# A chunked state-space layer with a mixture of experts on one core: the softplus and the spreading of the step sums move to GpSimd

## The reference

```python
h = quantised_table[x]                                   # 64 x 128 tokens, 192 wide
zxbcdt = layernorm(h) @ in_proj_w.T
dt = softplus(zxbcdt[..., -6:] + dt_bias)                # 6 heads
A_cum = cumsum(dt * -exp(A_log), axis=tokens)
Lmat = exp(A_cum[..., :, None] - A_cum[..., None, :])    # lower triangle
Y = (C @ B.T * Lmat) @ (x * dt) + D * x                  # per head
h = h + sigmoid(gate) * (rmsnorm(Y * silu(z)) @ out_proj_w.T) + layernorm(h)
out = h + experts(layernorm(h))
```

## Time and profile before

| | us |
|---|---|
| median of 3 runs | 1089.92 (1089.62 to 1092.22) |
| the profiled execution | 1093.7 |
| its span, first to last instruction | 1091.9 |
| TensorE busy | 941.4 |
| VectorE busy | 692.4 |
| ScalarE busy | 583.9 |
| GpSimd busy | 526.2 |

### The profile page before, as it was taken

One profiled execution on the slowest core, in us unless ns is written; L12 is line 12 of the kernel. 1 busy time (PEld: TensorE's weight loads), 2 busy tenths in 40 slices (PEclk: granted clock), 3 DMA queues, 4 the chain that ended last, 5 costly groups with the idle time before them and its releaser, 6 DMA issues.

```text
span 1091.9 us, 20110 instructions
## 1 busy us (share of the span) xinstructions
PE 941.4 (86%) x5743; PEld 613.0 (56%) x5744; DVE 692.4 (63%) x2047; ACT 583.9 (53%) x1195; POOL 526.2 (48%) x622
## 2 busy tenths in 40 slices
PE   0688898888988998898998879899989988889985
PEld 0234455455544554455455556677767666667774
DVE  3678998999989989899889433676651211212120
ACT  2657886778868777788675244233232232232330
POOL 6222435356354463551514427333447776775453
PEclk9889998999989899899897799999999999999997
DMA  4910011011101110010001212134331121222220
GB/s 107 319 43 10 16 44 42 5 46 45 44 3 45 44 47 30 18 45 30 25 9 55 66 33 77 51 98 123 112 83 47 53 61 43 55 59 70 69 59 22
DMA packets 50001, 61.53 MB, mean 56 GB/s; under 512 B 22525, under 2 KB 41689, under 8 KB 49413
## 3 DMA queue, kind: packets, MB, share of 16 engines
q0 software_dynamic: 16704, 30.54, 9.8%
q1 hardware_dynamic: 28580, 24.93, 7.5%
q10 hardware_dynamic: 4640, 5.13, 1.7%
HBM read 36.24 MB, written 25.92 MB: 57 GB/s over the span
## 4 chain that ended last, share of the span: by engine, by line
PE 40%; DVE 25%; issue 13%; ACT 12%; POOL 7%; DMA 2%; POOLq 1%; DVEq 0%; ACTq 0%
DVE xbc L1435 11%; PE cx L1219 6%; PE mm L1057 5%; PE yb L1219 4%; PE mm L1061 4%; PE mm L1207 4%; PE mm L1203 4%; PE sg L1203 3%; POOL out_dram L611 2%; PE sg L975 2%; DVE mix L1455 2%; ACT rows_s L747 2%; ACT h L694 2%; ACT xbc L722 2%; POOL list_u L576 1%
## 5 line engine op out<-in xcount | busy, mean ns | idle before, releaser
L1435 DVE SCALAR_TENSOR_TENSOR xbc<-mm,cw,xbc 128x508 f32<-128x508 f32 (+2 forms) x231 | 168.5, 741 | 31.8 <-ACT xbc L722 26.4
L1057 PE MATMUL mm<-xt_a,win_a 128*128 128x512 f32 x248 | 148.1, 681 | 35.7 <-DVE xbc L1435 26.7
L903 ACT ACTIVATE ht<-mm,b1s 128x256 f32<-128x256 f32 x102 | 44.7, 472 | 230.5 <-PE sg L1207 228.0
L592 POOL DMA_INDIRECT xg<-hr_dram,ids x80 | 81.3, 1016 | 80.3 <-DVE res L1762 44.3
L511 POOL TENSOR_TENSOR ybuf<-ybuf,zs 128x384 f32<-128x384 f32 x64 | 69.5, 1087 | 100.5 <-DVE ybuf L1468 100.5
L722 ACT ACTIVATE xbc<-mm,cb,cw 128x512 f32<-128x512 f32 x77 | 56.6, 775 | 108.6 <-PE mm L1061 108.6
L611 POOL DMA_INDIRECT out_dram<-osb,ids_s x80 | 81.7, 1021 | 64.3 <-DVE osb L1772 43.0
L1772 DVE TENSOR_TENSOR osb<-cx,res 128x192 f32<-128x192 f32 x40 | 14.2, 356 | 143.6 <-PE cx L1219 142.0
L1203 PE MATMUL mm<-fx_a,w1a_t 128*128 128x256 f32 x240 | 81.9, 424 | 13.7 <-issue 7.6
L1219 PE MATMUL cx<-w2s,ht 128*128 x408 | 86.8, 365 | 5.5 <-issue 5.2
L1207 PE MATMUL mm<-fx_b,w1b_t 64*128 64x256 f32 x240 | 85.3, 436 | 0.0
(11 more groups left out here) (273 smaller groups left out, 2068.6 us busy)
## 6 DMA issues: line engine op xcount, KB each, us to landing
hr_dram<-hr SPq DMA_DIRECT2D x16, 768.0 KB
w2s<-in_w2c_dram SPq DMA_DIRECT2D x4, 576.0 KB
w2s_u<-in_w2u_dram ACTq DMA_DIRECT2D x4, 576.0 KB
list_c<-fill SPq DMA_DIRECT2D x2, 1032.0 KB, 12.3
list_u<-fill SPq DMA_DIRECT2D x2, 1032.0 KB, 18.5
w1a<-in_w1c_dram SPq DMA_DIRECT2D x4, 384.0 KB
w1a_u<-in_w1u_dram ACTq DMA_DIRECT2D x4, 384.0 KB
xg<-hr_dram,ids POOLq DMA_INDIRECT x80, 3.1
```

The source lines that it names most:

```text
L592: nc.gpsimd.indirect_dma_start(out=xg[:, v, t, :], out_offset=None, in_=rows, in_offset=bass.IndirectOffsetOnAxis(ap=ids[:, v, t, 0:1], ax ...
L1057: mmul(tile_bank(g2, m)[:, :], win_a[:, column(m):column(m) + P], xt_a[:, p, :], start=True, stop=False)
L1435: ins = stt(out=dst_[:, :, back:L], in0=src[:, :, 0:L - back], scalar=cw[:, m, TAPS - 1 - back:TAPS - back], in1=dst_[:, :, back:L], op0=A ...
```

## The change

Two pieces of work go to GpSimd. ScalarE keeps `rows_t` and makes one row more, `rows_u` (the sums, or 1, in all blocks), earlier than before: ahead of `start(6)` and `start(7)`. GpSimd multiplies `rows_u` by a mask in `seg_c` and so fills `rows_s` in two halves (`spread_rows(0)` and `spread_rows(1)`), and `seg(j)` waits for the half that it needs. VectorE keeps the first two operations of the softplus (`soften`) and does them ahead of `residual(0)`; the other ones of the series and the four writes of `drep` are done by GpSimd, twelve operations in place of eight, since the fused ones are split.

```diff
@@ gpsimd
+                def spread_rows(q):
+                    pool.wait_ge(s_ru, g2 + 1)
+                    nc.gpsimd.tensor_tensor(rows_s[:, q, :, :], rows_u[:, :].unsqueeze(1).broadcast_to([P, HPB, P]),
+                                            seg_c[:, q * HPB:(q + 1) * HPB].unsqueeze(2).broadcast_to([P, HPB, P]),
+                                            ALU.mult).then_inc(s_rows, 1)
+                def softplus():
+                    pool.wait_ge(s_rec, g2 + 1)
+                    link(gp.tensor_tensor(S1, U, S2, ALU.mult))
+                    link(gp.tensor_tensor(S2, S1, S1, ALU.mult))
+                    link(gp.tensor_scalar(S3, S2, SERIES[-1], SERIES[-2], ALU.mult, ALU.add))
+                    for c in SERIES[-3::-1]:
+                        link(gp.tensor_tensor(S3, S3, S2, ALU.mult))
+                        link(gp.tensor_scalar(S3, S3, c, None, ALU.add))
+                    link(gp.tensor_tensor(S3, S3, S1, ALU.mult))
+                    link(gp.tensor_scalar(S2, x, 0.0, None, ALU.max))
+                    gp.tensor_tensor(dts[:, p, :, :], S2, S3, ALU.add).then_inc(s_dts, 1)
+                    pool.wait_ge(s_dts, g2 + 1)
+                    wait(pool, s_ct, g2)
...
+                    last.then_inc(s_dt, 1)
                 gate_y(0)
                 rms()
                 gate_y(1)
+                softplus()
                 if t + 2 < NG:
                     gather(t + 2)
                 gate_y(2)
                 norm2()
+                spread_rows(0)
                 gate_y(3)
+                spread_rows(1)
                 list_tokens()
@@ scalar
-                    for n in range(2 * HPB):
-                        last = nc.scalar.activation(rows_s[:, n // HPB, n % HPB, :], sums_, ACT.Identity,
-                                                    bias=seg_c[:, 1, n:n + 1], scale=seg_c[:, 0, n:n + 1])
-                    last.then_inc(s_rows, 1)
+                    nc.scalar.activation(rows_u[:, :], sums_, ACT.Identity, bias=seg_c[:, at + 3:at + 4],
+                                         scale=seg_c[:, at + 2:at + 3]).then_inc(s_ru, 1)
                 from_tp(g1, 1, 1)
+                sum_rows()
                 start(6)
                 start(7)
-                sum_rows()
@@ tensor
-                    pe.wait_ge(s_rows, g3 + 1)
+                    pe.wait_ge(s_rows, 2 * g3 + 1 + j // 2)
@@ vector
+                def soften():
+                    dve.wait_ge(s_u, g2 + 1)
+                    chains["head"](ts(sp1[:, :, :], dtu[:, g2 % 2, :, :], 2.0, None, ALU.add))
+                    v.reciprocal(sp2[:, :, :], sp1[:, :, :]).then_inc(s_rec, 1)
                 weights(2)
                 conv(4)
+                soften()
                 residual(0)
-                softplus()
                 y(2)
```

More of the change, by code:

```diff
@@ L73 @@
 ROWS = 32
-STEPS = dict(quant=2, clip=3, tap=10, soft=9, ssd=4, h1=2, pick1=1, pick2=8, find=6)
+STEPS = dict(quant=2, clip=3, tap=10, soft=11, head=1, ssd=4, h1=2, pick1=1, pick2=8, find=6)
 def wait(eng, sem, value):
@@ L298, in build @@
         s_dts, s_free = sem("dt_values"), sem("stage_a_done")
+        s_rec = sem("softplus_reciprocal")
+        s_ru = sem("step_sum_row")
         s_early = sem("early_units_listed")
@@ new lines, in softplus @@
+                def softplus():
+                    if g2 is None:
+                        return
+                    p, slot = g2 % 2, (t + 1) % 2
+                    gp, link = nc.gpsimd, Chain(pool, ch["soft"], g2, STEPS["soft"])
+                    U, S1, S2, S3 = dtu[:, p, :, :], sp1[:, :, :], sp2[:, :, :], sp3[:, :, :]
+                    x = sd[:, slot, :, DTR:DTR + HEADS]
+                    pool.wait_ge(s_rec, g2 + 1)
[8 more added lines that the diff above has]
+                    gp.tensor_tensor(dts[:, p, :, :], S2, S3, ALU.add).then_inc(s_dts, 1)
+                    link.end()
+                    pool.wait_ge(s_dts, g2 + 1)
+                    wait(pool, s_ct, g2)
+                    for jj in range(2):
+                        for rep in range(2):
+                            to = drep[:, :].rearrange("p (q b r) -> p q b r", q=2, b=2)
+                            r = 2 * HPB * jj + HPB * rep
+                            last = gp.tensor_tensor(to[:, :, :, r:r + HPB],
+                                                    dts[:, p, 2 * jj:2 * jj + 2, :].rearrange("p q (b h) -> p q b h", b=2),
+                                                    nega[:, :].rearrange("p (b h) -> p b h", b=2).unsqueeze(1).broadcast_to([P, 2, 2, HPB]),
+                                                    ALU.mult)
+                    last.then_inc(s_dt, 1)
@@ L1369, in body @@
                 chains = {n: Chain(dve, ch[n], g, STEPS[n]) for n, g in (
-                    ("soft", g2), ("tap", g2), ("ssd", g3), ("h1", g4)) if g is not None}
+                    ("head", g2), ("tap", g2), ("ssd", g3), ("h1", g4)) if g is not None}
                 b5, first5 = batch(g5) or (None, None)
@@ L1897, in sum_rows @@
         block = np.arange(2 * HPB)[None, :] == (r // (2 * HPB) * HPB + r % HPB)[:, None]
-        scale = np.concatenate([block * (rep == 0)[:, None], -(rep == 1)[:, None].astype(int)], axis=1)
-        bias = np.concatenate([block * (rep == 1)[:, None], (rep == 0)[:, None]], axis=1)
-        return (np.concatenate([scale, bias], axis=1) * used[:, None]).astype(np.float32)
+        first, second = (rep == 0)[:, None].astype(int), (rep == 1)[:, None].astype(int)
+        return (np.concatenate([block, -second, first, first, second], axis=1) * used[:, None]).astype(np.float32)
     def by_part(b):
```

38 lines of the change are left out of this document (10 added, 28 removed).

## The result

The changed kernel takes **1131.49 us** (median of 4 runs, 1128.24 to 1132.34) against 1091.07 for the kernel before on the same occasion: a ratio of 1.0356, with a 95% interval of 1.0332 to 1.038. It is 40 us slower. The profiled execution took 1128.24, with a span of 1126.5; the mean granted clock is the same as before, 0.944.

What follows compares the result with a forecast made beforehand. It took VectorE's row of work, closed into a ring by `seg(0)`, to bound stage A. Rerouted through GpSimd, the ring adds 34.4 us, with the clock 51: 1093.7 becomes 1144.7, median 3.8 lower, forecast 1141, range 1112 to 1166.

Steps and rivals of the forecast that it cites:

- parts 4 and 5: GpSimd's queue from softplus to spread sets `seg(0)`, interval 38.75 us against 35.66; the path over `drep` ends 2.3 us earlier.
- The softplus on GpSimd, 5.75 us: Twelve linked small operations at 0.34 us, four `drep` writes at 0.23, and 0.75 us of stall beside VectorE's `mix`.
- The gather, 5.55 us: GpSimd's fetch of embedding rows, from `gidx` to what follows, queued behind the softplus and ahead of `gate_y(2)`.
- the rival of the stretched gather: Gather held off entirely beside VectorE's y(3) and `clip`: 2.3 us times 12, 1169 us; chance 0.10.
- The back way, 15.55 us: From S to the next `seg(0)`: soften, hop, softplus, gather, gate, `norm2` and spread, 15.55 us in all.
- The front way, 23.2: From `seg(0)` to S: 23.88 us less 0.65, as VectorE's two kept operations go ahead of `residual(0)`.
- the clock's 1.85 us in nine intervals: TensorE idles some 4 us before each `seg(0)`, its clock falls: 1.85 us in nine of twelve intervals, 17 us.
- The last three intervals, -2.1: Stage A's last three iterations have no gather: 102.9 us against 105.0, so 2.1 us shorter.
- S: The moment at which VectorE is done with `conv(4)`, forecast at 23.2 us after `seg(0)`.
- the case of the clock that stays up: Rival: TensorE's clock does not fall at the longer waits, so only +34.4 us, 1124 us; chance 0.18.
- The dear operations: Rival: GpSimd's operations cost more (0.45 us linked, spread 1.7), 2.3 us times 12, 1168 us; chance 0.10.
- the cheap ones: Rival: GpSimd's linked operations take 0.22 us each, 1.7 us less an interval, about 1120 us; chance 0.07.

Runs made afterwards that it cites:

- gather_behind: The changed kernel with GpSimd's gather put behind both spreads and the list stores behind `norm1`; 1097.19 us, 1.0042 of the kernel before.
- pad_both: The changed kernel with three more 384-element GpSimd products into a scratch tile between softplus and gather; 1219.8 us, 1.0719 of the kernel before.
- changed_again: The changed kernel, unaltered, run once more on another chip; 1130.39 us, 1.0364 of the kernel before.

## Why the prediction was right, point by point

- **What bounds the kernel, and that the change closes a ring through GpSimd** (parts 4 and 5): right. The place, the releaser (`rows_s`) and the order of the stations stand in the trace; gather_behind and pad_both show it by subtraction and addition.
- **The softplus on GpSimd, 5.75 us**: 5.18 from 312.28. A link of the chain is 0.30 to 0.37 us where nothing stalls it, as taken (0.34). The stall beside `mix` is there as well (314.57, 0.81 in place of 0.24, beside the `mix` of 314.34), 0.57 and not 0.75.
- **The gather, 5.55 us**: 5.55, in part by luck. Of the 5.55 before, 0.20 was `gate_y(2)` waiting for VectorE; that wait is gone, and the fourth issue, now beside `clip`, takes 1.12 (321.87). Before it took 0.95:

```profile
477.44 0.95 POOL L485 DMA_INDIRECT gath<-in_table_dram,gidx  x1 [0.30 <-issue]
```

  It is so in eleven of the twelve intervals, and there `clip`'s second part takes 2.4 us (322.20) in place of 1.74. So the rival of the stretched gather came with 0.17 us and not 2.3. The Trainium skill ("SBUF — State Buffer", the box on SWDGE) has a DMA issue of GpSimd locked out while VectorE runs a two-port operation. The trace agrees at most in part: nothing here holds the issue off for the length of `clip`.
- **The back way, 15.55 us**: 14.40. The terms were each a little high: softplus 0.57, `norm2` 0.18, the spread with its hop 0.28. The spread takes 0.83 where 1.05 was taken from `gate_y`. The Trainium skill ("GPSIMD Engine Reference", section "Performance versus the Vector engine") gives about 2.6 cycles an element; at its 1.2 GHz that is 0.83 us for 384 elements, as an estimate. The spread agrees, while `gate_y`, whose row was used, is at 1.00, and the three products of pad_both are at 0.96 each. Over twelve intervals the back way is 12.3 us of the miss (12 x 15.55 - 1.5 against 12 x 14.40), the largest part.
- **The front way, 23.2, and the clock's 1.85 us in nine intervals** (24.6 on the mean): 24.00. The charge of 17 us was of the right size: 16.4 us in eight intervals. The term that was mis-sized is the base: 23.2 was read from one even iteration, and an undisturbed odd one takes 22.2, and so does the first, which makes 7 us less in twelve. That is nearly all of the 7.3 us by which this part was too long. What was also wrong is to call the charge a cost of the change. The 427.9 that the sum was set against holds falls already: the front way was 24.06 before and is 24.00 now, so all of the +32.9 lies in the back way. That a low base and a charge for the clock together came near 24.06 is luck.
- **The last three intervals, -2.1**: +1.9. This step was wrong, in sign too. Without a gather `rows_s` is early, and what ends last is TensorE's own list, from `step_sums`, which waits for `drep`, to `seg(0)`, which waits for nothing. TensorE, then GpSimd, in the first of the three:

```profile
549.91 0.49 PE L1030 MATMUL sg<-le,drep 128*128 128x128 f32 x2 [1.68 <-POOL drep L539]
...
556.67 0.91 PE L1020 MATMUL sg<-rows_s,rows_t 32*128 32x384 f32 x4
...
554.52 0.82 POOL L510 TENSOR_TENSOR rows_s<-rows_u,seg_c 128x384 f32<-128x384 f32 x1
```

  `rows_s` was ready at 555.34, 1.3 us ahead of `seg(0)`. The back ways are 12.64, 10.64 and 13.48, where the sum had 13.3, 10.0 and 10.0. This is the second ring: part 5 had its price by way of VectorE to `mix(0)` (S + 15.4), but not the branch that stays on TensorE (y(3), `prefixes` in every second iteration, `project(0)`, `cbx(0)`, `seg(0)`: 4.75 to 7.55 us from `step_sums`, the longest with projections of 1.77 and 2.03 us, at a clock of 0.62 from 618 to 622.5).
- **VectorE would wait 2.3 us ahead of `mix(0)`**: in the iteration shown it doesn't; `mix(0)` starts at S + 16.3, not S + 17.7, and the wait (1.08) stands before `conv(0)`. VectorE fills the time with `places`, in that iteration. In the even ones it waits 2.4 to 2.7 us ahead of y(3), and 1.1 us ahead of `mix(0)` in the one of 286.83, which is the predicted wait at another place.
- **Sum**: for the profiled execution 1144.7 was forecast and 1128.24 measured: 12.3 us too much in the back way and 7.3 in the front way, 4.0 too little in the last three, under 1 in the rest. The median, 1131.5, lies 3.3 above that execution, where the prediction took it to lie below as before; so the forecast of 1141 missed it by 9.5. Against the kernel before, +51 us were forecast; measured are +34.5 between the two profiled executions and +40 between the medians.
- **The rivals**: the case of the clock that stays up (1124) is nearer the result than the forecast, and for the profiled execution (1093.7 + 34.4 = 1128.1) it is the result. That is chance: its condition is not met, as the clock falls in eight of twelve front ways, and it hits because 12 us too much in the back way stand against 10 too little in the front way and 4 in the last three intervals. The dear operations and the cheap ones did not come, the gather was stretched by 0.17 us only, and the ring does not stay on VectorE.

## What to carry to other kernels

Work moved to an idle engine costs what stands between it and its reader in that engine's list: two moves that are each harmless closed a ring over a 5.5 us gather that had harmed nobody. Before such a change, write down the list of the receiving engine from the first moved instruction to the last one that another engine waits for, and move what nobody waits for behind it; then look for the next reader (here `step_sums`, with y(3) and TensorE's own way to `seg(0)` behind it). When a path is priced from an undisturbed iteration, compare it with an undisturbed one, not with a mean that already holds the disturbances, and take one of each kind where even and odd iterations differ.

## What the runs showed of the hardware

- Idle time of TensorE can cost more than itself: behind waits of 1.76 to 3.7 us for `rows_s`, matmuls often ran at about half speed (2.08 in place of 1.12 us), and matmuls without use, put into the wait, took 15.5 us off the kernel (1130.39 to 1114.89). It is not so each time: behind the wait of 1.76 at 327.74 in changed_again the clock was 0.73 (329 to 334); behind that of 1.76 at 326.16 in the first trace of the same kernel it was 1.00 (326 to 334).
- A chain of 24-element operations on GpSimd costs 0.30 to 0.37 us a link, of which the operation itself is 0.21 to 0.29. Beside VectorE's `mix` (0.95 us) one such operation took 0.81.
- The same kernel differed by 1.5% in its ratio to the same reference kernel between two chips, more than either interval (1.0026 to 1.0081 and 0.9879 to 0.9942). A 1% verdict from one chip is not one for all.
